# Where one tile's attention products stand in a group's program, on one core of a Trainium2 chip

## The reference, cut to what matters

```
q_phi, k_phi = elu(rope(q)) + 1, elu(rope(k)) + 1      # 16 heads of 8 numbers
M = M * b_t + k_t v_t ;  Z = Z * b_t + k_t             # per token, 2 decays per head
y_t = (q_t . M) / (q_t . Z + EPS)
x = x + ga * layernorm(h + y @ Wo + bo)
h = layernorm(x) * (1 + cb) + sb
logits = h @ router_w.T ; top 2 of 8 experts
rank = cumsum(onehot) - 1 ; keep = rank < capacity     # slot of each (token, expert) pair
buf[expert, slot] += h ; out = silu(buf @ w1) @ w2     # 8 experts of 128 x 512 x 128
x = x + gb * (sum of the two experts' rows, weighted, + h)
```

## Time and profile before

| | |
|---|---|
| median of 3 runs | 296.11 us (294.85 to 299.49) |
| the profiled execution | 293.68 us, its span 291.9 us |
| mean granted clock of PE | 0.886 of full speed |
| PE / weight loads / DVE / ACT / POOL busy | 251.4 / 188.4 / 209.2 / 121.2 / 90.0 us |
| body 0, 1, 2, 3 on PE (from start of scores or ranks) | 41.16, 78.08, 115.78, 154.65 us |
| last scatter issued, experts' first transpose | 191.92, 197.65 us |

### The profile page before, as it was taken

One profiled execution on the slowest core, in us unless ns is written; L12 is line 12 of the kernel. 1 busy time (PEld: TensorE's weight loads), 2 busy tenths in 40 slices (PEclk: granted clock), 3 DMA queues, 4 the chain that ended last, 5 costly groups with the idle time before them and its releaser, 6 DMA issues. The chain is left out here.

```text
span 291.9 us, 11345 instructions
## 1 busy us (share of the span) xinstructions
PE 251.4 (86%) x4731; PEld 188.4 (65%) x4731; DVE 209.2 (72%) x828; ACT 121.2 (42%) x274; POOL 90.0 (31%) x102
## 2 busy tenths in 40 slices
PE   7997898799977999899887889988999999999900
PEld 3665657676566855678555564436898889888800
DVE  5697989849699597986778568837557655756563
ACT  4598258652668444753322122203233432343200
POOL 0030014000023406052134216740544464546630
PEclk9999579779998799955999596999999999999965
DMA  6980000030700103000021001122424433331566
GB/s 178 338 311 4 3 2 6 4 146 4 291 4 4 30 3 112 13 4 12 22 80 46 21 6 57 45 80 86 129 55 130 147 96 108 121 100 36 172 214 227
DMA packets 18197, 25.19 MB, mean 86 GB/s; under 512 B 2679, under 2 KB 11400, under 8 KB 18146
## 3 DMA queue, kind: packets, MB, share of 16 engines
q1 hardware_dynamic: 14434, 19.18, 20.5%
q0 software_dynamic: 2368, 4.24, 4.5%
q10 hardware_dynamic: 1344, 1.05, 1.1%
HBM read 12.84 MB, written 12.15 MB: 86 GB/s over the span
## 5 line engine op out<-in xcount | busy, mean ns | idle before, releaser
L948 ACT ACTIVATE arena<-ps 128x385 f32<-128x385 f32 (+1 forms) x64 | 27.6, 439 | 62.3 <-PE ps L1876 61.6
L685 POOL DMA_INDIRECT pair_out<-arena,meta x40 | 39.2, 981 | 45.0 <-DVE arena L1407 19.2
L631 POOL DMA_INDIRECT dispatched<-row,idx x32 | 32.5, 1014 | 60.2 <-PE ps L1619 27.6
L1893 PE MATMUL ps<-w2t,arena 128*128 128x128 f32 x320 | 40.4, 278 | 0.0
L1893 PEld LDWEIGHTS ps<-w2t,arena 128*128 128x128 f32 x320 | 39.3, 191 | 0.9
L1512 PE MATMUL ps<-later_b,ident_b 128*128 128x512 bf16 x141 | 38.1, 409 | 0.0
L1876 PE MATMUL ps<-arena,w1t 128*128 128x256 f32 (+1 forms) x128 | 37.6, 434 | 0.2 <-issue 0.2
L1407 DVE SCALAR_TENSOR_TENSOR arena<-ps,meta,arena 128x128 f32<-128x128 f32 x40 | 14.0, 351 | 26.4 <-PE ps L1893 15.4
L654 POOL TENSOR_TENSOR arena<-arena,ex 128x256 f32<-128x256 f32 x16 | 10.7, 695 | 68.2 <-DVE arena L1029 50.2
L1612 PE MATMUL ps<-v,wts 32*32 32x9 f32 x2048 | 24.0, 180 | 8.8 <-issue 6.5
L1612 PEld LDWEIGHTS ps<-v,wts 32*32 32x32 f32 x2048 | 22.0, 117 | 13.5 <-issue 13.1
(11 more groups left out here) (182 smaller groups left out, 446.3 us busy)
## 6 DMA issues: line engine op xcount, KB each, us to landing
dispatched<-fill SPq DMA_DIRECT2D x12, 260.0 KB, 4.2
pair_out<-zero SPq DMA_DIRECT2D x6, 512.0 KB, 3.4
arena<-dispatched SPq DMA_DIRECT2D x8, 325.0 KB, 3.0
w1t<-in_w SPq DMA_DIRECT2D x8, 256.0 KB, 2.7
w2t<-in_w SPq DMA_DIRECT2D x8, 256.0 KB, 3.1
arena<-pair_out SPq DMA_DIRECT2D x4, 512.0 KB, 5.1
const<-in_constants SPq DMA_DIRECT2D x1, 803.5 KB, 6.5
X<-in_x SPq DMA_DIRECT2D x1, 768.0 KB, 7.6
```

Of the source, the lines that this page charges most:

```text
L631: pool.indirect_dma_start(disp_d, bass.IndirectOffsetOnAxis(ap=idx[:, p.g, t, k:k + 1], axis=0), row[:, p.g, t, k, :], None, bounds_check= ...
L685: pool.indirect_dma_start(pair_d, bass.IndirectOffsetOnAxis(ap=meta[:, u, a, 0:1].bitcast(U32), axis=0), orow[:, u, a, :], None, bounds_ch ...
L948: a_.activation(hid[:, u, f, c0:c0 + cn], ps[:, k % 4, 0:cn], ACT.Silu).then_inc(hid_done[u].sem, 1)
L1893: m = mm(row_bank(u, a)[:, 0:P], hid[:, u, f, 1 + a * P:1 + (a + 1) * P], w2t[:, u, f, :], start=(f == 0), stop=(f == FT - 1))
```

## The change

PE: `attention(g,1)` is the first thing in a body instead of following `exponents(n)`; it now comes right after the projections at the end of the body before, and ahead of `ranks`. In body 2, whose end has no projections, five `keep_streaming` products are taken out. DVE: `normed(g,0)` moves from body g to just before `choice` of the body before (for group 0, into the prologue); both halves of the rotary products are now ahead of `slot`, and `block_rates(n)` comes after `rotated(n)`. POOL: the scatters of a group are split 3, 2, 3 instead of 3, 3, 2, the middle two wait for `scores(n,0)`, and the last three for `attention(n,0)`; none waits for the end of `route` any longer.

```
@@ gpsimd
                     dispatch(whole(g - 1), 0, 3)
+                    pool.wait_ge(scored.sem, scored.now(g + 1, 1))
+                    dispatch(whole(g - 1), 3, 5)
                     pool.wait_ge(att_ps.sem, att_ps.now(g + 1, 1))
-                    dispatch(whole(g - 1), 3, 6)
-                    pool.wait_ge(h2_ps.sem, h2_ps.now(g))
-                    dispatch(whole(g - 1), 6, TG * TOPK)
+                    dispatch(whole(g - 1), 5, TG * TOPK)
@@ rope_products
-                    if n == 3 and hi == TG and g:
-                        block_rates(g)
@@ dve_body
                 if more:
                     rope_products(n, 0, TG // 2)
+                    rope_products(n, TG // 2, TG)
                 if g:
                     slot(whole(g - 1))
-                normed(g, 0)
                 if more:
-                    rope_products(n, TG // 2, TG)
                     rotated(n)
+                    block_rates(n)
@@ dve_body, before the choice; and in the prologue after clipped_logits(1)
                     mask_states(n, 1)
+                    normed(n, 0)
                     choice(whole(g))
...
             clipped_logits(1)
+            normed(0, 0)
@@ pe_body
                 n, m = g + 1, g + 2
+                attention(g, 1)
                 if g:
                     ranks(whole(g - 1))
...
                 if more:
                     exponents(n)
-                attention(g, 1)
                 adds(g, 3)
...
                     if m < GROUPS:
                         project(m, 1, TG)
-                    else:
-                        keep_streaming(ps[:, 0, :], 5)
```

## The result

The changed kernel takes 305.53 us (median of 4 runs, 302.4 to 308.83; a fifth took 301.16); the kernel before, run beside it, takes 295.48. The ratio is 1.026, with a 95% interval of 1.016 to 1.036: slower, while the interval leaves open whether by more than 2%. Runs over 1.5% above the fastest of the same kernel are left out of all ratios, and the profiled execution of after (308.83 us) is such a run, so that by the ratio the change costs 7.6 us, by the medians 10.1, and by the two profiles 15.1.

A forecast was written before the change was run, and what follows sets the result against it. A body was taken as DVE's chain plus two round trips by PE and ACT, with PE stalling for code. Terms +1.2 + 0.5 + 0 - 2.0 = -0.3 us on a profiled 293.68; median placed at 295.5, range 289 to 303.

The forecast's parts named there:

- Places of the boundaries: PE code boundaries some 21 and 149 products behind each body's head; last body's stall at `scores(3,2)`.
- the 1.7 taken: PE's stall for code at the head of `scores(g,2)`: 1.2 to 2.3 us, taken as 1.7.
- Code is there in time: Rival: code asked for during the projections arrives without a stall at the heads; -6.3 us, 289.8; chance 0.24.
- the other rival: Clock falls at body heads; 2.6 us a body, 303.3, if stall over about 1.5 and in all three bodies; chance 0.18.
- What that costs: Delay from the stall at the heads: +1.2 us in body 0, +0.5 in body 1, 0 in body 2.
- The last body, −2.0: Last body: DVE's own norm starts earlier, its 2.49 us idle mostly goes; 2.0 us gained, all reaching the end.
- The division, −0.65 a body: DVE: `normed(n,0)` fits the idle gap ahead of the choice; 0.65 us gained in each of bodies 1 and 2.
- `block_rates` behind `rotated` costs PE nothing: PE in `exponents`: the later `block_rates` delays nothing, and PE's 0.58 us wait goes.
- Scatters, 0: POOL's new scatter split: zero net effect, between -0.2 and +0.2 us a body.

The follow-up runs named there:

- x4: The changed kernel with 64 more products (128 instructions) issued ahead of the first body, shifting every code boundary: 309.51 us, ratio 1.047 to the kernel before.
- x2: The kernel before with only attention 1 moved to the body's head (five streaming products out) and the division early: 302.96 us, ratio 1.023.
- y1: The kernel before with the attention 1 move, without the five streaming products, and the early division in the last body only: 294.93 us, ratio 1.001.
- x5: The kernel before with only the division `normed(n,0)` put ahead of the choice: 292.94 us, ratio 0.993.
- x3: The changed kernel with seven streaming products as filler between attention 1's value and state products: 302.93 us, ratio 1.023 to the kernel before.
- z2: The kernel before with the early division, and attention 1 of groups 1 and 2 put between router and projections: 297.92 us, ratio 1.010.
- v2: The kernel before with the early division and `block_rates(n)` behind `rotated(n)`, attention 1 left in place: 300.87 us (4 runs), 296.43 for before in its job.
- x6: The kernel before with only the new split of the scatters (3, 2, 3): 295.40 us, ratio 1.001.
- run 128: Not a follow-up run or kernel: "run" is a verb here, in stretches that execute 128 short products in 1.25 us; no time or ratio belongs to it.
- x1: The changed kernel with PE's program of the kernel before put back: 297.10 us, ratio 1.003 to the kernel before.

## Why the prediction was wrong, point by point

**Places of the boundaries: right in bodies 0 to 2, not in the last.** In the profiled run the heads of bodies 0 to 2 stand with nothing waited for, 1.2 to 1.8 us for the 1.7 taken; in body 1 the gap is 149 products behind the head, as counted, in body 0 three products later and in body 2 two ahead of the attention's end; and x4 moved the gap by the count. In the last body no gap stands at `scores(3,2)`, in after, x2 and y1 alike: in x2 and y1 attention 1 ran there at the low clock (2.19 us for its value products), and so it was in x2's body 0 (1.90, gap 0.19). The two gaps of after's last body don't lie at counted places, and their cause is open. The stalls go against the sentence of the Trainium skill ("Runtime: NRT & Kernel Launch", Instruction fetch mechanics) that fetching is mostly hidden; the 16 KiB blocks of that section agree with 0.61 MB in 37 packets.

**"Code is there in time": fell**, by the same gaps. (Its 289.8 was counted from 296.1, the other rival's 303.3 from 295.5.)

**"What that costs", +1.2, +0.5 and 0: this is the step that failed.** Measured in the profiled run: +3.9, +7.5 and +2.7 us (x2 over x5: +2.6, +6.0 and +3.2). The paragraph followed the delay down body 1, and so can the traces; times are us behind the body's choice:

| body 1 | transposes behind ranks | DVE's sums | `queries_T` | own norm | next choice |
|---|---|---|---|---|---|
| before | 2.9 | 6.3 | 13.0 | 24.9 | 37.7 |
| predicted | 6.1 | 8.0 | 13.5 | | 38.2 |
| after | 6.5 | 9.6 | 16.7 | 29.6 | 45.2 |
| x2 | 6.8 | 10.1 | 17.1 | 30.4 | 43.2 |
| x3 | 7.1 | 9.4 | 14.9 | 28.3 | 41.1 |

The times are read from the profiled executions; x2 has the DVE order of before. The late head was right: attention 1's own 1.6 us and the stall were both in it. Wrong was how much of it would reach `queries_T`: 0.5 us predicted, 3.7 measured. x3, whose head ran at full clock, tells what the low clock did to that: with a head that is later still it reaches `queries_T` 1.8 us later than before, close to what the paragraph gives for such a head (about 1.5). After loses 0.8 us to x3 between the transposes and the sums and 1.6 between the sums and `queries_T`. So 2.4 us of the missed 3.2 go with the clock, which the sum left at nothing and gave to a rival.

The rival had this mechanism and came out at 303.3; I gave it 0.18 against 0.50. Of its condition the fall in all three bodies came true in the profiled run, though body 0's gap was 1.22 us and not over 1.5; in x2 the clock was low at the heads of bodies 0 and 1 and not of body 2. The pauses between bursts of products that the Trainium skill ("TensorE: Matmul & The Clock Gate", HAM oscillation) names are there at the heads of bodies 0 to 2 of after, so the trace agrees with it; in z2's body 2 the clock fell at attention 1 with no idle time of PE over 0.44 us in the four us before. "What the engine did before it fell" in the earlier trace rows was the same attention, but the same attention in body 1 of before was followed by the full clock (79 to 86 above), so that row gave a reason for a larger chance and no certainty. How much of the whole loss is stall, clock and the products' own time isn't settled; each of the heads above has at least two of the three.

**The loss doesn't end with the head.** I took the rest of the body as it was. From `queries_T` to the own norm after needs 1.0 us more than before, x2 1.4 and x3 1.6, all with another low stretch of the clock in it (103 to 110, 98 to 108 and 97 to 107 us); DVE's wait ahead of the own norm grew from 3.18 to 4.31 us in after. And after's last part needs 2.9 us more, under a third low stretch (117 to 124), which x2 and x3 don't have.

**The last body, −2.0: wrong.** I looked at the idle 2.49 ahead of the own norm and not at ranks, which now stand behind attention 1: y1 waits 1.88 us there (2.77 in after, 0.38 before) and gains nothing. The stall that was to fall on `scores(3,2)` didn't come; the clock was low from attention 1 on (153.4 in y1, 167.9 in after) instead.

**The division, −0.65 a body: right.** x5 gained 2.7 us by the medians and 0.7% by the ratio, with 0.2 to 1.1% as its interval, in which the 1.3 us lie. Body 1 gave 0.6, about the term; body 2 gave 2.2 in the profiled pair, but there x5 also had less of the low clock (13.7 us for 17.1), so not all of it need be the division's.

**"`block_rates` behind `rotated` costs PE nothing": not so by itself.** v2 has 1.22 us of wait there. In the changed kernel PE was late anyway, and the wait didn't show.

**Scatters, 0: right** (x6, 1.001).

## What to carry to other kernels

Count the instructions of the engine with the most of them, mark where its code pieces end, and keep stretches that run 128 short products in 1.25 us away from work that another engine waits for: in the old place the gaps stood where DVE had other work. When a block of sparse products is moved, follow the delay step by step to what waits for it, and do so a second time with the steps at the low clock, if a row shows the clock low behind such a block even once. Separate a bundled change early; here the one small part that helped was worth 0.7%, and the rest took 3.2 points.

## What the runs showed of the hardware that I had not expected

PE's idle time for code is no measure of the loss. In the profiled executions, between 40 and 170 us the gaps with nothing waited for come to 5.5 us in before, 6.1 in x2, 6.8 in x5, 8.7 in after, 11.8 in x1 and 12.7 in x4; x1, with 11.8, takes 297.1 us, and x2, with 6.1, takes 303.0. x1's lie in `scores(g,3)`, attention 2 and later, where DVE has its own long stretch; x1's body 1 is 1.2 us longer than before's for 2.6 us more of them. Nor is the granted clock: the two executions with the highest mean, x3 (0.910) and v2 (0.919), took 303.69 and 299.87 us, and x5, with 0.893, took 291.87.

The stall and the low clock seem to work against each other. Where attention 1 ran at the low clock (x2's body 0, value products in 1.90 us), the gap at the next counted boundary was 0.19 us; where it ran at full clock (x2's body 1, 1.25 us) it was 2.11. In the last bodies of x2 and y1 (2.19 us) there was none. These are four heads, and no run was made to test it.
